# Strassen's seven block products for the q and k projections of a head pair

## What is computed

```python
def ffn(x):        # 64 experts of rank 16, top 16 of them per token
    h = einsum('nd,krd->nkr', x, A)
    return 2.0 * einsum('nkr,kdr->nd', h * G[:, :, None], B)   # G: gates
def attention(x):  # 32 heads; 4 sequences of 256 tokens; first 128 channels of q
    q, k, v = x @ wq, x @ wk, x @ wv
    probs = softmax(causal(q @ k.T * 192 ** -0.5))
    return (probs @ v) @ wo
x = x + 0.5 * ffn(layernorm(x))
x = x + attention(layernorm(x))
x = x + 0.5 * ffn(layernorm(x))
```

## Time and profile before

| what | us |
|---|---|
| median of 3 timed runs | 1134.2 |
| lowest and highest of them | 1133.47 and 1136.23 |
| span of the profiled execution | 1133.8 |

### The profile page before, as it was taken

The page is one execution under the profiler, slowest core; times in us unless marked ns, Lnnn a source line. Parts: engine busy times, 40 slices in busy tenths (PEclk is TensorE's granted clock), DMA queues, the critical chain, the costliest instruction groups (busy, mean ns, idle before and its releaser), DMA issues.

```text
span 1133.8 us, 19445 instructions
## 1 busy us (share of the span) xinstructions
PE 1119.3 (99%) x6708; PEld 1004.5 (89%) x6708; DVE 601.3 (53%) x1780; ACT 401.1 (35%) x1297; POOL 249.5 (22%) x191
## 2 busy tenths in 40 slices
PE   7999999999999999999999999999999999999998
PEld 7899888888888888888888888888888888888997
DVE  6775444545454545454545454545454545465553
ACT  4121343333333333333333333333333333331110
POOL 5310140404040404040403131313131313010000
PEclk8999999999999999999999999999999999999999
DMA  7010010101010101010101020202020201000000
GB/s 264 1 37 1 20 56 20 57 19 55 18 55 18 55 18 55 18 56 18 58 16 62 12 70 4 74 0 74 0 74 1 73 2 53 1 1 1 28 19 28
DMA packets 12613, 42.36 MB, mean 37 GB/s; under 512 B 1328, under 2 KB 1328, under 8 KB 12592
## 3 DMA queue, kind: packets, MB, share of 16 engines
q1 hardware_dynamic: 12592, 42.08, 10.7%
HBM read 39.98 MB, written 2.10 MB: 37 GB/s over the span
## 4 chain that ended last, share of the span: by engine, by line
PE 95%; DVE 2%; DMA 1%; ACT 1%; issue 0%; SPq 0%; POOL 0%; DVEq 0%
PE bank L177 28%; PE bank L179 28%; PE bank L178 28%; PE bank L290 4%; PE bank L280 2%; PE bank L304 2%; PE bank L218 1%; DMA x<-x_in 1%; DVE xa L450 0%; PE bank L185 0%; PE bank L241 0%; ACT prob L383 0%; DVE xn L450 0%; DVE st L442 0%; DVE hT_lo L437 0%
## 5 line engine op out<-in xcount | busy, mean ns | idle before, releaser
L177 PE MATMUL bank<-xnT_lo,wqk_hi 128*128 128x512 f32 x512 | 205.7, 402 | 0.0
L179 PE MATMUL bank<-xnT_hi,wqk_hi 128*128 128x512 f32 x512 | 200.0, 391 | 0.0
L178 PE MATMUL bank<-xnT_hi,wqk_lo 128*128 128x512 f32 x512 | 199.3, 389 | 0.0
L179 PE MATMUL bank<-wv_hi,xnT_hi 128*128 128x256 f32 x512 | 144.9, 283 | 0.0
L178 PE MATMUL bank<-wv_hi,xnT_lo 128*128 128x256 f32 x512 | 144.9, 283 | 0.0
L177 PE MATMUL bank<-wv_lo,xnT_hi 128*128 128x256 f32 x512 | 144.6, 282 | 0.0
L383 ACT ACTIVATE prob<-prob,nmax 128x128 f32<-128x128 f32 (+1 forms) x256 | 113.5, 445 | 62.4 <-DVE nmax L521 62.4
L437 DVE TENSOR_TENSOR kT_lo<-bank,kT_hi 128x512 fp32r<-128x512 f32 x64 | 44.3, 692 | 155.4 <-ACT kT_hi L352 155.4
L179 PEld LDWEIGHTS bank<-xnT_hi,wqk_hi 128*128 128x128 f32 x512 | 96.1, 188 | 21.2
L555 DVE TENSOR_TENSOR x<-bank,x 128x512 f32<-128x512 f32 x128 | 88.0, 688 | 47.4 <-PE bank L179 47.4
L178 PEld LDWEIGHTS bank<-xnT_hi,wqk_lo 128*128 128x128 f32 x512 | 96.4, 188 | 15.8
(11 more groups left out here) (102 smaller groups left out, 2322.8 us busy)
## 6 DMA issues: line engine op xcount, KB each, us to landing
stage_qk<-wqk SPq DMA_DIRECT2D x32, 512.0 KB, 3.4
stage_vo<-wv SPq DMA_DIRECT2D x16, 512.0 KB, 4.4
stage_vo<-wo SPq DMA_DIRECT2D x16, 512.0 KB, 3.3
upT_raw<-up_w SPq DMA_DIRECT2D x4, 544.0 KB, 7.1
downT_raw<-down_w SPq DMA_DIRECT2D x4, 512.0 KB, 10.5
out<-x SPq DMA_DIRECT2D x8, 256.0 KB, 2.0
x<-x_in SPq DMA_DIRECT2D x1, 1536.0 KB, 14.2
x<-x_in SPq DMA_DIRECT2D x2, 256.0 KB, 6.0
```

Of the source, the lines that this page charges most:

```text
L177: nc.tensor.matmul(dst, a_hi, b_lo, start=first, stop=False)
L178: nc.tensor.matmul(dst, a_lo, b_hi, start=False, stop=False)
L179: return nc.tensor.matmul(dst, a_hi, b_hi, start=False, stop=last)
```

## The change

The q projection of a pair, and the k projection too, is one product of a 512 x 256 weight with 512 x 1024 inputs. Cut in halves along all three directions it is a 2 x 2 by 2 x 2 block product, before eight block products of 6 matmuls with 512 columns each (256 channels of depth, 128 of one head, 512 tokens), now seven, by Winograd's form of Strassen's scheme. The text calls them M1 to M7, as the functions `pe_m1` to `pe_m7`. Their operands are sums: four of the weights, made by POOL in `pool_w_operands` for each pair and for q and k apart (S1, S3, S2, S4, each 128x256), and four of the inputs, made once (T1, T2, T3, N4) by DVE in `dve_att_transposed_half1` and `dve_combined` with a cast on ACT. The results C11, C21, C22, C12 are put together partly in PSUM (M6, M5, M3 add onto M1 in one bank, M4 adds onto M7 in `yz`), partly by copies that ACT takes of intermediate states (`act_snap1`, `act_snap2`, `act_snap7`) and DVE adds. The order of units is now (head 0, half 0), (head 1, half 0), (head 1, half 1), (head 0, half 1).

All of a pair's products are now issued during the pair before, so pair 0's stand before the pairs, and the last pair has none. The split operands, seven weights each for q and k and eight inputs, need room in SBUF, so the split FFN weights are written to DRAM during the first FFN (four transfers, 8.65 MB) and read back to other addresses in the last pair.

```diff
+B11, B21, B12, B22, T1, T2, T3, N4 = range(8)
+S3, A11, A12, A22, S1, S2, S4 = range(7)
...
+        keep_up = [nc.dram_tensor(f"keep_up{i}", [P, KD * UPW], F32, kind="Internal").ap() for i in range(2)]
+        keep_down = [nc.dram_tensor(f"keep_down{i}", [P, NR * D], F32, kind="Internal").ap() for i in range(2)]
...
-        def pe_project(pe, j, qk, dst, done):
-            head, half = j % 2, j // 2
-            for k in range(KD):
-                last = mm3(dst[:, :], wqk_hi[:, head, qk, k, :], wqk_lo[:, head, qk, k, :],
-                           xnT_hi[:, k, half * HALF:(half + 1) * HALF],
-                           xnT_lo[:, k, half * HALF:(half + 1) * HALF], k == 0, k == KD - 1)
-            last.then_inc(done, 1)
+        def product(g, dst, w, c, onto):
+            for k in range(2):
+                mm = mm3(dst[:, :], w_hi[g][:, w, k * P:(k + 1) * P], w_lo[g][:, w, k * P:(k + 1) * P],
+                         xc_hi[:, c, k, :], xc_lo[:, c, k, :], k == 0 and not onto, k == 1, onto)
+            return mm
+        def pe_m1(pe, g, p):
+            pe.wait_ge(s[f"w{g}_split"], 2 * p + 1)
+            if not isinstance(p, int) or p > 0:
+                pe.wait_ge(s[f"{g}_split"], 4 * p)
+            product(g, acc[g], A11, B11, False).then_inc(s[f"{g}x_ready"], 1)
+        def pe_m2(pe, g, p):
+            if g == "k":
+                pe.wait_ge(s["q_split"], 4 * p + (2 if not isinstance(p, int) or p > 0 else 1))
+            elif not isinstance(p, int) or p > 0:
+                pe.wait_ge(s["k_split"], 4 * p - 2)
+            product(g, yz, A12, B21, False).then_inc(s[f"{g}y_ready"], 1)
+        def pe_m6(pe, g, p):
+            pe.wait_ge(s[f"{g}_snap"], 3 * p + 1)
+            product(g, acc[g], S2, T2, True).then_inc(s[f"{g}x_ready"], 1)
+        def pe_m7(pe, g, p, free=None):
+            if free is not None:
+                pe.wait_ge(s[free[0]], free[1])
+            else:
+                pe.wait_ge(s[f"{g}_split"], 4 * p + 1)
+            product(g, yz, S3, T3, False).then_inc(s[f"{g}y_ready"], 1)
+        def pe_m4(pe, g, p):
+            pe.wait_ge(s[f"{g}_snap"], 3 * p + 3)
+            product(g, yz, A22, N4, True).then_inc(s[f"{g}y_ready"], 1)
+        def pe_m5(pe, g, p):
+            pe.wait_ge(s[f"{g}_snap"], 3 * p + 2)
+            product(g, acc[g], S1, T1, True).then_inc(s[f"{g}x_ready"], 1)
+        def pe_m3(pe, g, p):
+            pe.wait_ge(s[f"w{g}_split"], 2 * p + 2)
+            pe.wait_ge(s[f"{g}_sum"], 3 * p + 3)
+            product(g, acc[g], S4, B22, True).then_inc(s[f"{g}x_ready"], 1)
...
-                pe_scores(pe, u, j)
-                nj = (j + 1) % 4
-                project = not (final and j == 3)
-                if project:
-                    if nj == 0:
-                        pe.wait_ge(s["wqk0_split"], p + 2)
-                    if nj == 1:
-                        pe.wait_ge(s["wqk1_split"], p + 1)
-                    if first and nj == 2:
-                        pe.wait_ge(s["xaT_split"], NT)
-                    pe_project(pe, nj, 0, qp, s["q_ready"])
+                if not (first and j == 0):
+                    pe_scores(pe, u, j)
+                if not final:
+                    if j == 0:
+                        pe_m1(pe, "q", p + 1)
+                        pe_m2(pe, "q", p + 1)
+                    elif j == 1:
+                        pe_m4(pe, "q", p + 1)
+                        pe_m1(pe, "k", p + 1)
+                    elif j == 2:
+                        pe_m5(pe, "q", p + 1)
+                        pe_m7(pe, "k", p + 1)
+                    else:
+                        pe_m3(pe, "q", p + 1)
+                        pe_m5(pe, "k", p + 1)
...
-                if project:
-                    pe_project(pe, nj, 1, kp, s["k_ready"])
+                if not final:
+                    if j == 0:
+                        pe_m6(pe, "q", p + 1)
+                        pe_m7(pe, "q", p + 1)
+                    elif j == 1:
+                        pe_m2(pe, "k", p + 1)
+                        pe_m6(pe, "k", p + 1)
+                    elif j == 2:
+                        pe_m4(pe, "k", p + 1)
+                    else:
+                        pe_m3(pe, "k", p + 1)
...
+        def act_snap1(act, g, p):
+            act.wait_ge(s[f"{g}x_ready"], 4 * p + 1)
+            if g == "k":
+                act.wait_ge(s["q_sum"], 3 * p + 1)
+            elif not isinstance(p, int) or p > 0:
+                act.wait_ge(s["k_sum"], 3 * p - 2)
+            act_copy(s1[:, :], acc[g][:, :]).then_inc(s[f"{g}_snap"], 1)
+        def act_snap2(act, g, p):
+            act.wait_ge(s[f"{g}x_ready"], 4 * p + 2)
+            if g == "k":
+                act.wait_ge(s["q_sum"], 3 * p + 2)
+            elif not isinstance(p, int) or p > 0:
+                act.wait_ge(s["k_sum"], 3 * p - 1)
+            act_copy(s2[:, :], acc[g][:, :]).then_inc(s[f"{g}_snap"], 1)
+        def act_snap7(act, g, p):
+            act.wait_ge(s[f"{g}y_ready"], 3 * p + 2)
+            if not isinstance(p, int) or p > 0:
+                act.wait_ge(s[f"{g}_split"], 4 * p - 1)
+            act_copy(s7[g][:, :], yz[:, :]).then_inc(s[f"{g}_snap"], 1)
+        def act_c11(act, g, p):
+            act.wait_ge(s[f"{g}_sum"], 3 * p + 1)
+            act_rounded(g, 0, yz[:, :])
...
-                act_exp(act, u)
-                if not (final and j == 3):
-                    act_q(act, u + 1, nj % 2)
+                if not (first and j == 0):
+                    act_exp(act, u)
+                if not final:
+                    if j == 0:
+                        act_snap1(act, "q", p + 1)
+                        act_c11(act, "q", p + 1)
+                    elif j == 1:
+                        act_c21(act, "q", p + 1)
+                        act_snap1(act, "k", p + 1)
+                    elif j == 2:
+                        act_c22(act, "q", p + 1)
+                        act_snap7(act, "k", p + 1)
+                    else:
+                        act_c12(act, "q", p + 1)
+                        act_c22(act, "k", p + 1)
...
+        def dve_att_transposed_half1(dve, t):
+            h = t - TH
+            cols = slice(h * P, (h + 1) * P)
+            b12, b22 = half1_raw[:, 0, :, cols], half1_raw[:, 1, :, cols]
+            t1, t2, t3, n4 = (comb_raw[:, i, :, cols] for i in range(4))
+            n = 6 * h
+            def f32(tile, i):
+                return tile[:, i, :, cols].bitcast(F32)
+            dve.wait_ge(s["xaT_hi_done"], t + 1)
+            nc.vector.tensor_tensor(t1, b12, f32(xc_hi, B11), ALU.subtract).then_inc(s["comb_step"], 1)
+            nc.vector.tensor_tensor(t3, b22, b12, ALU.subtract).then_inc(s["comb_step"], 1)
+            dve.wait_ge(s["comb_step"], n + 1)
+            nc.vector.tensor_tensor(t1, t1, f32(xc_lo, B11), ALU.subtract).then_inc(s["comb_step"], 1)
+            dve.wait_ge(s["comb_step"], n + 3)
+            nc.vector.tensor_tensor(t2, b22, t1, ALU.subtract).then_inc(s["comb_step"], 1)
+            dve.wait_ge(s["comb_step"], n + 4)
+            nc.vector.tensor_tensor(n4, f32(xc_hi, B21), t2, ALU.subtract).then_inc(s["comb_step"], 1)
+            lo(xc_lo[:, B12:B22 + 1, :, cols].rearrange("p i k t -> p (i k) t"),
+               half1_raw[:, :, :, cols].rearrange("p i k t -> p (i k) t"),
+               xc_hi[:, B12:B22 + 1, :, cols].rearrange("p i k t -> p (i k) t")).then_inc(s["xaT_split"], 1)
+            dve.wait_ge(s["comb_step"], n + 5)
+            nc.vector.tensor_tensor(n4, n4, f32(xc_lo, B21), ALU.add).then_inc(s["comb_step"], 1)
...
+        def dve_low(dve, g, p, i, src):
+            dve.wait_ge(s[f"{g}_hi_done"], 4 * p + i + 1)
+            lo(unit_tile(lo_t, g, i), to_split(src, g), unit_tile(hi, g, i)).then_inc(s[f"{g}_split"], 1)
+        def dve_c11(dve, g, p):
+            dve.wait_ge(s[f"{g}y_ready"], 3 * p + 1)
+            wait_alone(dve, s[f"{g}_snap"], 3 * p + 1)
+            nc.vector.tensor_tensor(yz[:, :], yz[:, :], s1[:, :], ALU.add).then_inc(s[f"{g}_sum"], 1)
+            dve_low(dve, g, p, 0, yz[:, :])
...
+        def dve_c22(dve, g, p):
+            dve.wait_ge(s[f"{g}x_ready"], 4 * p + 3)
+            wait_alone(dve, s[f"{g}_snap"], 3 * p + 3)
+            nc.vector.tensor_tensor(s7[g][:, :], acc[g][:, :], s7[g][:, :], ALU.add).then_inc(s[f"{g}_sum"], 1)
+            dve_low(dve, g, p, 2, s7[g][:, :])
...
+        def pool_w_operands(pool, g, p):
+            i = 2 * p + KIND[g]
+            pool.wait_ge(s["w_loaded"], 16 * (i + 1))
+            n = 4 * i
+            def add(out, a, b, op, after):
+                if after:
+                    pool.wait_ge(s["w_sum_s"], n + after)
+                nc.gpsimd.tensor_tensor(stage_w[:, out, :], stage_w[:, a, :], stage_w[:, b, :],
+                                        op).then_inc(s["w_sum_s"], 1)
+            add(S1, A21, A22, ALU.add, 0)
+            add(S3, A11, A21, ALU.subtract, 0)
+            add(S2, S1, A11, ALU.subtract, 1)
```

(62 more changed lines are left out.)

371 lines of the change are left out of this document (241 added, 130 removed).

## The result

| kernel | median, us | lowest to highest |
|---|---|---|
| before | 1133.85 | 1133.47 to 1136.23 |
| with the change | 1143.96 | 1143.37 to 1145.13 |

The ratio is 1.008 (95% interval 1.0068 to 1.0092): 0.8% slower, where 1125.5 and faster was forecast. It lies inside the range (1111 to 1147), close to the first rival's 1147. The profiled execution has a span of 1143.2, 9.4 more than before.

What follows compares the result with a forecast made beforehand. The prediction took PE's own work as the bound (busy 99% of the span). Its terms, -43.6 + 12.8 + 17.0 + 1.0 + 4.0 = -8.8 us, gave a median of 1125.5 us, range 1111 to 1147.

Steps and rivals of the forecast that it cites:

- first rival: Unit j = 2: POOL's large cast comes between the normalisations, PE waits 2.3 us per pair, 1147 us in all; chance 0.25.
- Term 1: Fewer matmuls for q and k: 84 in place of 96 per pair, 2.73 us less each, -43.6 us over 16 pairs.
- Term 2: One new PE wait per pair, at k's M4 in j = 2: 0.85 us in 15 pairs, +12.8 us.
- The rival with 2.3 per pair: Unit j = 2: POOL's cast also falls before the last normalisation, so PE waits about 2.3 us; 1147 us, chance 0.25.
- Term 3: New PE waits ahead of the pairs and around pair 0's products, with 2.0 us for a lower clock: +17.0 us.
- the first `xa`: Ahead of the pairs, near 80 us: a normalisation held behind POOL's split of k's weights, PE waiting about 2.1 us.
- tile 6's: Ahead of the pairs: tile 6's `xa` stands behind six more DVE instructions and PE comes 1.4 us sooner; 2.7 us of waiting.
- Term 4: Pair 0, no output fill in j = 1: 2.73 us less covers the chains, about 1.0 us more waiting.
- Term 5: Last pair: without products the softmax is not covered and PE waits; net +4.0 us.
- The parked weights: FFN weights written to DRAM in the first FFN (8.65 MB) and read back in the last pair: no cost.
- the long wait: Unit j = 2: the large cast between the normalisations makes PE wait 2.3 us per pair, 1147 us; chance 0.25.
- the forecast's own case: Unit j = 2: two normalisations held about 0.65 us each, one PE wait of 0.85 us per pair, 1125.5 us; chance 0.57.

Runs made afterwards that it cites:

- second experiment: The changed kernel with only POOL's cast of 1536 and what follows it begun after the softmax normalisations, the four sums unmoved: 1122.37 us, ratio 0.9895 to the kernel before.
- first experiment: The changed kernel with all POOL work on a pair's q weights begun only after the four normalisations of unit j = 2: 1116.24 us, ratio 0.9839 to the kernel before.

## Why the prediction was wrong

- **Term 1 held.** Without the new wait a pair takes 53.5 us.
- **Term 2 failed, and decided the sign.** The place was right (k's M4 in j = 2), the mechanism too (POOL's sums beside the normalisations, ACT's copy of M7 behind C22), and the size was not: 1.80 per pair, not 0.85. The step that failed is "two normalisations are held for about 0.65 each". All four were, each by one POOL instruction: three by sums of 0.74 (estimated at 0.6, from a longer one in proportion), the last by the cast of 1.47. I had written that the cast begins at 5.3 us of the unit or later and took this as speaking against it. But my own end of the held normalisations was 6.0 to 6.3, behind that. The cast began at 308.07 - 302.43 = 5.6, and the last normalisation was still to come. In an alternating queue each hold pushes the next instruction into the reach of the next one; I should have walked all four through. An estimate with my own durations: sums from 2.8 in steps of 0.6, the cast from 5.2 to 6.8, the normalisations behind them until about 4.0, 4.6, 5.2 and 6.8; that is 2.1 past the free end of 4.7, and with half a microsecond of room a wait of 1.6. The second experiment measures what is left without the cast (0.59), the first shows 0 without any. The rival with 2.3 per pair was the right case, its price too high by 0.5. One thing went the other way: POOL makes no q weights in pair 14, so 14 pairs wait and not 15. One reading was off, without effect on the sum: the second normalisation of the kernel before began at 217.60, 0.05 us behind POOL's subtraction and not just before it.
- **Pair 0 lost more to the same hold.** Its unit j = 2 gives back 4.40 without it (first experiment), where 0.85 was forecast: the wait itself, and the clock of 0.76 that followed it there. With 13 x 0.95 more in the other pairs and 0.85 less in pair 14, term 2 makes about 15 of the miss of 18.3.
- **Term 3 held in its sum, partly by luck.** +17.0 was forecast and about 16.9 came: 2.1 and 10.3 in the first two stretches of the table, and 0.57 + 2.46 of waiting with 1.5 of clock in the third. The single waits came out at 2.31 for the first `xa`, 2.37 for tile 6's, 1.11 for q's C11, 4.68 at the scores, 0.57 for M7 of k, 2.46 for k's C22 (M3 of k). The last five are 11.2 where 12.9 was forecast. The clock cost more than the 2.0 forecast: 1.6 behind the first wait (24 down matmuls 7.18 us, 5.56 before), about 1.7 up to the scores (0.94 in 28.85 us) and 1.5 up to k's C22 (0.92 in 18.44 us). And the first stretch hides that the steps ahead of the first wait had run 2.1 sooner, which is no more than the start varies by.
- **Term 4 held**, 1.0 forecast: its waits in pair 0 are 0.27 and 1.20, where 0.28 and 0.61 stood before.
- **Term 5 was too small**, 6.8 and not 4.0. The waits came out below the forecast: 0.27, 2.98 for the softmax and 0.72 for the copy of the probabilities, less the 0.27 and 0.61 of before, are 3.1. What was missing is the clock after them, which I had charged only ahead of the pairs; the last pair's unit j = 2 took 8.31 us where I had written 7.5. Windows of pair 0's unit j = 2, of a whole pair later on, and of the last pair from the scores of j = 3 (columns as in the earlier trace rows):

```profile
189.19:206.44 17.25, 14.85 (x94) 13.45 (x93) 10.61 (x23) 6.59 (x22) 6.72 (x5) 0.90 0.01 1
...
302.43:357.75 55.32, 53.98 (x334) 48.12 (x333) 35.07 (x94) 25.20 (x82) 24.58 (x21) 1.00 0.12 38
...
1018.84:1024.51 5.67, 5.67 (x24) 4.91 (x24) 3.63 (x16) 2.49 (x9) 0.00 (x0) 0.67 0.56 236
```

  5.67 us of work at 0.67 of full clock are 1.9 us lost. The 4.00 us ahead of them, from 1014.84, show 0.62: 1.5 more. In the later pair the wait of 1.80 left the clock at 1.00.
- **The parked weights cost nothing**, as forecast, and the second FFN waited for none.
- The chances: the long wait had 0.25, and the forecast's own case 0.57. With term 2's arithmetic done over four turns, the rival would have been the likeliest.

## What to carry to other kernels

Where two engines take turns at a shared resource, walk every instruction of both queues through, one after the other: a held instruction is still in the queue when the next long one comes. Saved matmuls pay only where every copy and sum that feeds the next one has slack; when a chain is put behind a softmax, look at what the idle engine beside it runs at that time, and begin that work when the chain has passed (one wait was worth 27 us here). At the ends of a loop, where the cover is missing, count the wait and the lower clock after it. And where two versions differ by 2 us or less, compare their profiles from a common instruction on: here the start alone moved by that much.
